# One image's w_out moved among the set matmuls of the next: a depthwise-convolution block on one core

## The reference

```
h = group-normalised x1                                  # per image and channel
h = einsum('oc,bchw->bohw', w_in, h)                     # 32 -> 170 channels
h = irfft2(rfft2(8x8 patches of h) * fft_filter)         # per channel, patch by patch
y = depthwise 3x3 convolution of h, padding SAME         # over the patches' borders too
g = gelu(y[:, :85]) * y[:, 85:]
out = x1 + einsum('oc,bchw->bohw', w_out, g)             # 85 -> 32 channels
```

## Time and profile before

| | us |
|---|---|
| median of 3 runs (3439.81 to 3449.4) | 3443.94 |
| span of the profiled execution, first to last instruction | 3457.4 |
| PE busy | 2908.9 (84%) |
| DVE busy | 1847.5 (53%) |
| ACT busy | 1311.5 (38%) |
| POOL busy | 253.1 (7%) |
| w_in of image 0 starts at | 1182.24 |
| w_in of image 1 starts at | 1250.12 |
| w_in of image 31 starts at | 3362.33 |

### The profile page before, as it was taken

One profiled execution on the slowest core, in us unless ns is written; L12 is line 12 of the kernel. 1 busy time (PEld: TensorE's weight loads), 2 busy tenths in 40 slices (PEclk: granted clock), 3 DMA queues, 4 the chain that ended last, 5 costly groups with the idle time before them and its releaser, 6 DMA issues.

```text
span 3457.4 us, 164388 instructions
## 1 busy us (share of the span) xinstructions
PE 2908.9 (84%) x74374; PEld 2020.6 (58%) x74374; DVE 1847.5 (53%) x4198; ACT 1311.5 (38%) x2217; POOL 253.1 (7%) x274
## 2 busy tenths in 40 slices
PE   4699999999996788888888888888888888888887
PEld 4355554555453666666666666666656666666665
DVE  3356565565652245554556555655555555555555
ACT  1234444444342233343434343433433333443332
POOL 2011111111110200000000000000000000000000
PEclk9899999999998599999999999999998999999999
DMA  6578778787764334334443444334433444334433
GB/s 126 124 170 172 164 169 170 172 171 165 165 144 69 32 100 111 95 93 104 117 106 89 107 119 105 89 99 105 116 97 89 105 115 112 89 99 113 113 92 84
DMA packets 451958, 404.16 MB, mean 117 GB/s; under 512 B 404172, under 2 KB 404478, under 8 KB 447497
## 3 DMA queue, kind: packets, MB, share of 16 engines
q1 hardware_dynamic: 446030, 376.93, 47.5%
q10 hardware_dynamic: 5228, 16.70, 1.4%
HBM read 165.77 MB, written 78.16 MB: 71 GB/s over the span
## 4 chain that ended last, share of the span: by engine, by line
PE 49%; DVE 6%; issue 5%; ACT 3%; DMA 3%; ACTq 2%; SPq 1%; POOL 0%; DVEq 0%; POOLq 0%
PE ps L1295 12%; PE ps L1245 10%; PE ps L1280 10%; PE ps L1309 9%; PE ps L1263 8%; DMA neighbours<-border 3%; DVE gated L1356 3%; ACT gelu L1180 2%; DVE channels_first L1369 2%; ACTq L1190 2%; ACT hidden_patches L1153 1%; DVE border L1163 1%; SPq L1052 1%; ACT border L1163 0%; DMA x_normed<-in_L_conv_w_in_dram 0%
## 5 line engine op out<-in xcount | busy, mean ns | idle before, releaser
L1356 DVE TENSOR_TENSOR gated<-gelu,ps 128x432 f32<-128x432 f32 (+1 forms) x512 | 289.3, 567 | 555.8 <-ACT gelu L1180 529.7
L449 ACT ACTIVATE hidden<-ps,hidden_scale 128x576 f32<-128x576 f32 x512 | 351.7, 738 | 614.5 <-PE ps L554 614.5
L1369 DVE STREAM_TRANSPOSE channels_first<-gated 128x512 f32<-128x512 f32 x576 | 571.3, 1043 | 1.1
L1153 ACT COPY hidden_patches<-ps 128x704 f32<-128x704 f32 x576 | 406.5, 749 | 434.3 <-PE ps L1245 434.2
L1280 PE MATMUL ps<-hidden_patches,channel_tables 64*64 64x144 f32 x11264 | 403.4, 287 | 97.4 <-DVE gated L1356 97.4
L1263 PE MATMUL ps<-hidden_patches,channel_tables 64*64 64x144 f32 x11264 | 405.7, 287 | 90.2 <-DVE border L1163 84.8
L568 PE MATMUL ps<-hidden,taps 128*32 128x288 f32 x6144 | 437.3, 417 | 43.1 <-DMA taps<-conv_tables 29.7
L1245 PE MATMUL ps<-w_in_t,x_normed 32*64 32x88 f32 x18432 | 422.3, 259 | 54.2 <-issue 49.3
L1263 PEld LDWEIGHTS ps<-hidden_patches,channel_tables 64*64 64x64 f32 x11264 | 359.4, 134 | 184.6 <-ACT border L1163 114.7
L1163 ACT COPY border<-ps 128x432 f32<-128x432 f32 (+1 forms) x512 | 226.4, 495 | 618.9 <-DVE border L1163 216.9
L554 PE MATMUL ps<-x_rows,taps 32*64 32x288 f32 x12288 | 455.0, 415 | 2.5 <-issue 1.3
(11 more groups left out here) (147 smaller groups left out, 1328.7 us busy)
## 6 DMA issues: line engine op xcount, KB each, us to landing
neighbours<-border SPq DMA_DIRECT2D x1024, 126.8 KB
taps<-conv_tables SPq DMA_DIRECT2D x192, 216.0 KB
x_image<-in_x_dram SPq DMA_DIRECT2D x128, 288.0 KB, 5.8
x<-x_image SPq DMA_DIRECT2D x128, 288.0 KB, 4.7
x_image<-x SPq DMA_DIRECT2D x384, 96.0 KB
out_dram<-x_image SPq DMA_DIRECT2D x384, 96.0 KB, 2.0
x_rows<-in_x_dram SPq DMA_DIRECT2D x512, 60.0 KB
neighbours<-border ACTq DMA_DIRECT2D x1024, 15.8 KB
```

The lines of the kernel that those rows point to most:

```text
L449: A(hid[T % 3][:, 2 * h:2 * h + 2, :, 1:1 + W], ps1[:, 2 * h:2 * h + 2, 0:XB * W].rearrange("p c (k w) -> p c k w", k=XB), ACT.Relu, scale ...
L1153: nc.scalar.copy(o, i).then_inc(s_we[pair], 1)
L1356: TT(o, gl[odd][:, 0:n * NPC].rearrange("p (t m) -> p t m", m=NPC), ps[:, 2 * odd + 1, 0:n * NPC].rearrange("p (t m) -> p t m", m=NPC), AL ...
L1369: last = nc.vector.transpose(t[:, s], g)
```

## The change

Only the second part changes.

* `w_in_step` does all four row groups of a step at once and uses two groups of four banks in turn, 4 to 7 and 0 to 3. Its 18 copies per image are split: 12 on ACT, 6 on DVE.
* Transposes, w_out and residual of image k-1 stand among the sets of image k, at places that the table `W_OUT` gives; w_out uses banks 4 and 5. `gated` has two buffers, and `channels_first` shares memory with `xn`, so POOL normalises the next image only after the last w_out of the one before.
* A set's border is done in two halves (`odd` 0 and 1), each into banks 6 and 7. The second half waits until the first one's two banks are copied. ACT copies all four, except that DVE takes one bank of each half in an image's first set.
* SP issues the corner moves as well in sets 2 to 7; ACT keeps those of sets 0 and 1. Each store and load of a third stands behind a set's moves, in the sets 2 to 7. A third of an image is waited for by itself, by POOL and by the residual.

```diff
+        W_OUT = [[0], [1], [2, 3], [4, 5], [6], [7], [8], [], [], []]
+        BANK_IN, BANK_OUT, BANK_EDGE = (4, 0), 4, 6
+        VEC_PAIRS = range(1, 2 * NW, 3)
...
             def move(S):
                 b = S % 2
-                sp.wait_ge(s_pe[0], S + 1)
-                sp.wait_ge(s_pe[1], S + 1)
+                border_copied(sp, 2 * S + 1)
                 need(sp, s_y, 2 * (S - 1))
                 for a in range(4):
                     f = EDGE + SIDE_SHIFT[a]
                     sp.dma_start(bd[b][a:P:8, :], be[b][a:P:8, f:f + RUN]).then_inc(s_b[b], 16)
+                if S % NSETS >= 2:
+                    for j in range(4):
+                        f, r = EDGE + CORNER_SHIFT[j], 8 * j + 4
+                        sp.dma_start(bd[b][r:P:NV, :], be[b][r:P:NV, f:f + RUN]).then_inc(s_bc[b], 16)
...
                 for s in range(NSETS):
-                    move(NSETS * k + s)
-                    if s == 1 and k > 0:
-                        store(k - 1, 2)
-                    if s == 3 and k > 0 and k + 1 < B:
-                        load(k + 1, 2)
+                    if s + 2 < NSETS:
+                        move(NSETS * k + s + 2)
+                    if k > 0 and s in (2, 4, 6):
+                        store(k - 1, (s - 2) // 2)
+                    if k > 0 and k + 1 < B and s in (3, 5, 7):
+                        load(k + 1, (s - 3) // 2)
...
+            for k in range(B):
+                for p in ACT_PAIRS:
+                    w_in_copy(act, nc.scalar.copy, k, p).then_inc(s_we[0], 1)
+                S = NSETS * k
+                edges(S, 0)
+                edges(S, 1)
+                move_corners(S)
+                edges(S + 1, 0)
+                edges(S + 1, 1)
+                move_corners(S + 1)
+                for s in range(NSETS):
+                    gelu(S + s, 0)
+                    gelu(S + s, 1)
+                    if s + 2 < NSETS:
+                        edges(S + s + 2, 0)
+                        edges(S + s + 2, 1)
...
+            def w_in_step(k, v):
+                pe.wait_ge(s_xn, 3 * k + v // 3 + 1)
+                if v >= 2:
+                    w_in_copied(pe, k, 2 * (v - 2) + 1)
...
+                if v == 1:
+                    need(pe, s_m, 2 * NSETS * k)
...
+            def border(S, odd):
...
+                if S > 0 or odd > 0:
+                    border_copied(pe, 2 * S + odd - 1)
...
+                border(S, 0)
+                border(S, 1)
+                hidden(S)
+                border(S + 1, 0)
+                for v in outs[0]:
+                    w_out_step(k - 1, v)
+                border(S + 1, 1)
+                for s in range(NSETS):
+                    add_neighbours(S + s)
+                    if s + 2 < NSETS:
+                        border(S + s + 2, 0)
+                    for v in outs[s + 1][:1]:
+                        w_out_step(k - 1, v)
+                    if s + 2 < NSETS:
+                        border(S + s + 2, 1)
+                    for v in outs[s + 1][1:]:
+                        w_out_step(k - 1, v)
+                    if s + 1 < NSETS:
+                        hidden(S + s + 1)
```

More of the change, by code:

```diff
@@ L973, in filter_part @@
         xn = sb("x1_normed", [P, PXQ])
+        ct = [xn[:, 1024 * i:1024 * i + 1024] for i in range(2)]
         sel = sb("select", [P, NV])
@@ L1157, in border_copy @@
             b, n = S % 2, SETS[S % NSETS]
[L1158 removed]
+            eng.wait_ge(s_p, 2 * S + odd + 1)
             need(eng, s_b[b], S // 2 * NMOVE * 16)
             need(eng, s_bc[b], S // 2 * NMOVE * 16)
[L1161 to L1163 removed]
@@ L1164, in border_copy @@
-            last.then_inc(s_pe[part], 1)
+            o = be[b][:, EDGE:EDGE + RUN].rearrange("p (i u r c) -> p i u r c", i=4, u=SLOTS, r=PADR)
+            return copy(o[:, 2 * odd + y, 0:n, 0:NPR, 0:NPR],
+                        ps[:, BANK_EDGE + y, 0:n * NPC].rearrange("p (u r c) -> p u r c", u=n, r=NPR))
         @block.scalar
@@ L1246, in w_in_step @@
                                       start=True, stop=True)
-                last.then_inc(s_w, 1)
-            def border(S):
+                        if i == WSTEP - 1 and q % 2 == 1:
+                            last.then_inc(s_w, 1)
+            def border(S, odd):
                 k, s = divmod(S, NSETS)
[L1252 to L1264, removed]
+                if s == 0 and odd == 0:
+                    w_in_copied(pe, k, 2 * NW - 1)
+                if S > 0 or odd > 0:
+                    border_copied(pe, 2 * S + odd - 1)
+                for m in range(CUT[s], CUT[s + 1]):
+                    o = (m - CUT[s]) * NPC
+                    for y in range(2):
+                        j = NT4 * y + 2 * m + odd
+                        for h in range(2):
+                            last = MM(ps[half(h ^ y), BANK_EDGE + y, o:o + NPC], tbl[half(h), j, NV:2 * NV], U[half(h), j, :],
+                                      start=True, stop=True)
@@ new lines, in _ @@
+            for k in range(B):
+                for p in VEC_PAIRS:
+                    w_in_copy(dve, TC, k, p).then_inc(s_we[1], 1)
+                S = NSETS * k
+                outs = W_OUT if k > 0 else [[]] * len(W_OUT)
+                border_copy(dve, TC, S, 0, 1).then_inc(s_pe[1], 1)
+                border_copy(dve, TC, S, 1, 1).then_inc(s_pe[1], 1)
+                for v in outs[0] + outs[1]:
+                    transposes(k - 1, v)
+                for s in range(NSETS):
+                    gate(S + s, 0)
+                    gate(S + s, 1)
+                    for v in (outs[0] if s == 0 else []) + outs[s + 1][:1]:
+                        residual(k - 1, v)
+                    for v in outs[s + 2][:1]:
+                        transposes(k - 1, v)
+                    for v in outs[s + 1][1:]:
+                        residual(k - 1, v)
+                    for v in outs[s + 2][1:]:
+                        transposes(k - 1, v)
@@ L1402 @@
+            for v in range(NW):
+                transposes(B - 1, v)
+                if v > 0:
+                    residual(B - 1, v - 1)
+            residual(B - 1, NW - 1)
 _INS = ["x", "L0_conv_fc0_w", "L0_conv_fc0_b", "L0_conv_fc1_w", "L0_conv_fc1_b", "L0_conv_w1", "L0_conv_b1",
```

142 lines of the change are left out of this document (54 added, 88 removed).

## The result

The changed kernel takes 3645.3 us (median, 3634.0 to 3649.9), the kernel before 3446.7 beside it: 1.059 times [1.0565, 1.0615], or 199 us more. The profiled execution's span is 3641.3 us against 3457.4 (+183.9). The forecast was 3500 us (3330 to 3600): the right sign, and less than a third of the size.

The account below looks back on a forecast made before the run. Before, PE was busy in w_in/w_out (25.75 us) and ring-bound in the sets (43.80). After, the ring through SP gives 71.6 us plus 1.0 for the clock, 72.6 against 70.41 an image; with the ends +56, so 3500 us (3330 to 3600).

Parts of the forecast that it names:

- The copies set the pace either way: w_in stretch: ACT's 12 of 18 copies take 8.4 us, so the stretch needs 10.4 us instead of 25.75.
- The step of 0.6 us: w_in alone: each of nine steps over four row groups takes 0.6 us, between 1.17 and half of that.
- the third rival: Whole image: SP is never waited for, PE and ACT bind; 65.2 us an image, 3285 us, chance 0.15.
- SP decides the second half: Sets behind the third border: four moves and three load/store groups run without slack on SP, 27.8 us; PE's adds wait.
- rival 1: SP's queue: it issues faster, 4.6 us a move; -1.8 us an image, 3385 us, chance 0.14.
- 80 issues of about 0.6 us are near the length of an image: SP's queue: issue times count whatever the transfers take, against the skill's rule that the issuing engine matters little.
- The sets with w_out: Sets: a period takes 6.1 us with one w_out step, 7.1 with two.
- The opening and the clock: Last w_in copy to second add: 15.9 us; TensorE's clock adds 1.0 us an image, range 0 to 5.
- the gelu behind ACT's corners: Opening: ACT's corner issues delay the gelu, so the second add at 15.9 us counts, not the first at 8.4.
- The prediction's own sign for a heavier clock: Opening: a PE row lasting twice its length would mean the clock counts for more than the forecast gave it.
- The ends: First and last images: image 0 62.5 us against 67.9 (-5), image 1 even (70), the last -3.
- Rival 2: SP and opening: a corner costs as much as a side, 5.8 us a move, half clock throughout; 3630 us, chance 0.11.

Follow-up runs that it names:

- both causes taken out: Changed kernel with all corner moves on ACT and half as many w_in matmuls, each twice as wide: 3356.19 us, 0.968 of the kernel before.
- The first experiment: Changed kernel with all corner moves back on ACT's queue, the rest as changed: 3538.99 us, 1.027 of the kernel before.
- the swap: Changed kernel with corners of sets 0 and 1 on SP and those of sets 2 to 7 on ACT: 3534.70 us, 1.027 of the kernel before.

## Why the prediction was wrong

**The failed step: "The copies set the pace either way: ACT keeps 12 of 18, two take 1.40 us, so 8.4 us."** PE's instruction supply sets it: 16.2 us instead of 10.4 (11.95 where the third load was to end it). That is 4.3 us an image, more than the whole excess over the forecast (76.3 against 72.6), and 6.6 us in image 0. With half the matmuls the stretch is 11.7 us, near those 11.95, so what was missing is the supply. The step of 0.6 us was short too: the first three took 3.64 us, 1.2 each, with the clock at 0.50 for most of that time. In sum w_in is 4.3 us over the forecast, the opening with its clock term 0.7 over (17.6 against 15.9 + 1.0), and the rest 1.2 under. The sign of it stood in the earlier trace rows, 48.1 us at "issue"; I took it as 1.6 us of stalls, and only in the third rival. Held against counts it was a rate. In the timeline of before:

```profile
2039.75 0.85 PE L1309 MATMUL ps<-channels_first,w_out_t 128*32 128x128 f32 x21 [0.40 <-issue]
...
2047.09 0.68 PE L1245 MATMUL ps<-w_in_t,x_normed 32*64 32x88 f32 x22 [1.05 <-issue]
```

Between these two stalls lie 7.34 us and 255 recorded matmuls of both lines, two periods. The old stretch of 864 matmuls needs 6.75 x 3.6 = 24.3 of its 27.2 us for supply. By this estimate, taking 288 w_out matmuls out of it could save 8.1 us and what is left of the old waits (2.9), not 15. The sets pay for the w_out steps in full: with both causes taken out, a period with two w_out steps is still 7.2 to 7.3 us where it was 4.8.

**SP decides the second half: right, at a lower price.** The sequence behind the third border is all but gapless, PE waits up to three us per add at the end, 196 us in all. Forecast 27.8 us, measured 25.9 in the rows above: four corners cost 2.06 (the lower bound was 2.0, I took 2.4). Three of the four moves took 4.5 us, under the 4.6 of rival 1, and PE waited for SP all the same. The prediction's "80 issues of about 0.6 us are near the length of an image" was loose: that is 48 us of 70, and it is the middle price, not the shortest, as rival 3 has it. The first experiment shows what they cost where it counts: 3.3 us an image. The rule cited, the Trainium skill, "DMA: Bandwidth & Descriptors", section "Issuing engines are not separate DMA queues", that issuing elsewhere saves only a small time, is not borne out by that run: 24 issues an image moved from SP to ACT are 106 us.

**The sets with w_out: right.** Periods forecast 7.1, 7.1, 6.1; measured 7.19, 7.18, 6.01.

**The opening and the clock: too short, and the runs point to the clock.** 15.9 us to the second add, measured 17.6 (10.44 + 7.12), and 20.0 in image 0. All of the excess lies ahead of the first add (forecast 8.4, measured 10.44); the gap behind it was forecast longer (7.5) than it is. The step named as decisive, "the gelu behind ACT's corners", is not what makes it long, as the swap showed. The prediction's own sign for a heavier clock is there, a PE row of the opening at nearly twice its length: hidden in the opening, at a granted clock of 0.50, and in a later set of the same image, at 1.00,

```profile
2183.87 3.14 PE L1304 MATMUL ps<-hidden_patches,channel_tables 64*64 64x144 f32 x48
...
2203.52 1.70 PE L1304 MATMUL ps<-hidden_patches,channel_tables 64*64 64x144 f32 x48
```

and the two half borders ahead of the first add (2256.75 and 2259.27) are busy for 1.7 us each where a later one is for 0.97. Ordered by the mean granted clock of the opening, the runs of the new order line up: 0.97 with half the matmuls, 16.2 us; 0.91 with half and corners on ACT, 16.7; 0.90 with the wider ones, 16.9; 0.82 as changed, 17.6; 0.80 to 0.81 in the other three, 17.7 to 17.8. No edit changed the clock alone, so this is an order among runs and not a proof. It puts the clock's price in the opening near 1.5 us an image, against the 1.0 of the forecast. For the whole time the clock is a small term: with the wider matmuls the mean is 0.931 instead of 0.899 (0.953 before), the opening is 0.7 us shorter, the w_in stretch 0.7 longer, and the time the same.

**The ends.** Image 0 was forecast 62.5 us and took 74.1: w_in 6.6, the opening 4.1, the rest 0.9. With 29 images at 3.7 above the forecast (108 us), image 1, forecast even (6.4), image 0 (11.2 in the difference to before), and some 2 us of the other ends, this is the 128 us between +56 and +183.9. Rival 2 came close to the time (3630) by luck: its corner price was 2.9 where 2.06 was measured, and w_in, the step that failed, was 10.4 us in it as well.

## What to carry to other kernels

A wait at "issue" that returns after a fixed number of matmuls is a rate: multiply it by the matmuls of a stretch before crediting the stretch with what the copies would allow, and try fewer, wider matmuls first (no run here did that with the reference's output). Count the DMAs that an engine must issue in a row against the time until their readers need them. Work moved into a busy ring costs its full length unless it goes exactly where the ring waits.

## What was not expected of the hardware

In the long w_in stretches PE took in f32 matmuls of 88 or 176 columns at about 127 per 3.5 to 4.1 us, at a granted clock of 0.60 as at 0.94, though a packet of 16.4 KB with their instructions takes 1.1 us: the rest is 1.4 us from its end to PE's next matmul and some 1.2 us from there to the next packet. A corner on SP took 0.482 us (median, had 0.610 on ACT while SP issued too), a side 0.589.
